# Last attention of a four-layer block on one core: the two heads of a unit are scored half a unit apart, each in banks of its own

## The reference, cut to what matters

```python
sim = jnp.einsum('bhid,bhjd->bhij', q * DIM_HEAD ** -0.5, k)      # 1024 x 1101 for a head
sim = jnp.where(full_mask[:, None, None, :], sim, max_neg)
attn = jax.nn.softmax(sim, axis=-1)
out = jnp.einsum('bhij,bhjd->bhid', attn, v)
out = layer_norm(jnp.einsum('bne,ed->bnd', out, Wout), g_o, b_o)
```

## Time and the profile before

| what | value |
|---|---|
| median of 3 runs | 2089.75 us (2084.55 to 2089.76) |
| profiled execution | 2084.4 us, its span 2082.6 us |
| last attention (first to last exponential) | 1099.6 to 1967.2 us of the span |
| TensorE busy in the span | 92% |
| VectorE, ScalarE, GpSimd busy in the span | 69%, 47%, 36% |

### The profile page before, as it was taken

How to read it: one execution, slowest core, us unless ns; L and a number is a source line. 1 busy time by engine, 2 the same in 40 slices (tenths; PEclk the granted TensorE clock), 3 DMA queues, 4 the chain that set the end, 5 groups by cost and what they waited for, 6 DMA issues and landing times.

```text
span 2082.6 us, 33216 instructions
## 1 busy us (share of the span) xinstructions
PE 1921.5 (92%) x11797; PEld 1355.2 (65%) x11797; DVE 1435.7 (69%) x2676; ACT 978.5 (47%) x2079; POOL 752.3 (36%) x1145
## 2 busy tenths in 40 slices
PE   6997799696999988997878999999999999998999
PEld 3885799542699976883565666666675666655644
DVE  5775111467344457787867999999878999998755
ACT  5672333343111252226875555555545555555455
POOL 1002111000522200000006777777656777777500
PEclk9897899898999999998989999999999999999999
DMA  3702899502489960002002333333222333333201
GB/s 115 208 2 79 273 323 333 170 1 86 163 292 321 310 228 1 1 1 86 1 13 60 82 83 82 83 83 83 72 57 72 82 82 82 82 82 81 63 1 41
DMA packets 191184, 226.87 MB, mean 109 GB/s; under 512 B 28939, under 2 KB 167085, under 8 KB 191021
## 3 DMA queue, kind: packets, MB, share of 16 engines
q1 hardware_dynamic: 183725, 201.98, 33.0%
q0 software_dynamic: 7296, 22.78, 3.3%
HBM read 127.64 MB, written 29.91 MB: 76 GB/s over the span
## 4 chain that ended last, share of the span: by engine, by line
PE 45%; ACT 6%; DVE 3%; issue 1%; POOL 0%; ACTq 0%; DVEq 0%; POOLq 0%
PE ps L640 41%; ACT w_odd L1796 4%; PE ps L1214 2%; PE ps L1215 1%; ACT arena L1785 1%; PE ps L1106 0%; DVE w_odd L2532 0%; DVE small L2410 0%; POOL arena L1908 0%; ACT out_feat L1708 0%; PE ps L1115 0%; ACT xn_tok L1651 0%; DVE small L2522 0%; ACT out_feat L1714 0%; DVE arena L2380 0%
## 5 line engine op out<-in xcount | busy, mean ns | idle before, releaser
L1908 POOL COPY arena<-w_odd 32x512 f32<-32x512 f32 x1024 | 623.7, 609 | 254.4 <-DVE w_odd L2532 202.1
L640 PE MATMUL ps<-arena,w_odd 128*128 128x128 f32 (+4 forms) x2352 | 468.2, 441 | 3.0 <-DVE arena L2202 1.2
L640 PE MATMUL ps<-arena 128*64 128x256 f32 (+4 forms) x3248 | 392.3, 370 | 8.3 <-DVE arena L2333 4.4
L640 PEld LDWEIGHTS ps<-arena 128*64 128x64 f32 (+4 forms) x3248 | 258.9, 155 | 119.5 <-issue 22.6
L2532 DVE STREAM_TRANSPOSE w_odd<-w_odd 128x1024 f32<-128x1024 f32 x256 | 317.4, 1245 | 14.6 <-ACT w_odd L1796 3.0
L1796 ACT ACTIVATE w_odd<-ps,small 128x1101 f32<-128x1101 f32 x256 | 301.6, 1179 | 48.0 <-DVE small L2522 41.0
L640 PEld LDWEIGHTS ps<-arena,w_odd 128*128 128x128 f32 (+3 forms) x2352 | 286.3, 188 | 27.9 <-issue 18.7
L1781 ACT ACTIVATE arena<-ps 77x256 f32<-77x256 f32 x128 | 48.5, 379 | 295.4 <-PE ps L1215 295.4
L2522 DVE TENSOR_REDUCE small<-ps 128x1 f32<-128x1101 f32 x128 | 166.9, 1304 | 29.3 <-PE ps L640 28.1
L1893 POOL DMA_INDIRECT token_rows<-arena x62 | 59.8, 964 | 292.3 <-DVE arena L2223 292.3
L2523 DVE TENSOR_REDUCE small<-ps 128x1 f32<-128x1024 f32 x128 | 155.4, 1214 | 0.0
(11 more groups left out here) (398 smaller groups left out, 2909.8 us busy)
## 6 DMA issues: line engine op xcount, KB each, us to landing
arena<-w_odd SPq DMA_DIRECT2D x1024, 64.0 KB
w_odd<-in_s_w SPq DMA_DIRECT2D x32, 1024.0 KB, 7.4
w_odd<-in_s_wgu SPq DMA_DIRECT2D x30, 704.0 KB, 6.1
w_even<-in_s_w SPq DMA_DIRECT2D x15, 1024.0 KB, 7.3
arena<-expert_rows_in SPq DMA_DIRECT2D x62, 130.0 KB, 4.7
w_odd<-in_s_wd SPq DMA_DIRECT2D x30, 256.0 KB, 3.6
out_feat<-in_s_wgu SPq DMA_DIRECT2D x10, 704.0 KB, 5.9
expert_rows_in<-zero_row POOLq DMA_DIRECT2D x1, 5070.0 KB, 33.2
```

The lines of the kernel that those rows point to most:

```text
L640: return pe.matmul(o, lhsT, rhs, start=start, stop=stop, **kw)
L1908: pool.tensor_copy(s6_d[u % 4][32 * j:32 * j + 32, :, 256 * i:256 * i + 256], s6_pm[u % 2][32 * i:32 * i + 32, :, 256 * j:256 * j + 256]). ...
```

## The change

- Scores: `scores(u, h)` for one head. Head 0 takes banks 0 to 2, head 1 banks 3 to 5. A head's 1024 keys now lie as 512 in partitions 0 to 63 and 512 in 64 to 127, so one head alone fills both row halves of the array. For this the queries are needed with their halves exchanged too (`s6_qs`), which SyncE makes by two DMAs for each query piece. The query tile has one buffer, no longer two.
- Mask: a matmul of ones with the mask (over the other 64 partitions) starts the sum of the 77 columns, and the context matmul adds to it. VectorE's addition and the split maximum go; it takes one maximum over 1101 columns for each head.
- Order on TensorE: head 0's scores; two pieces (odd units) or the first five tiles of `weigh` (even units); `ctx_turn(u - 1)`; head 1's scores; the last four tiles of `weigh` (even) or `sums_turn` (odd). Head 1's scores wait only for head 1's last exponential, head 0's for head 0's.
- Order on VectorE: maximum of head 0; turn of head 1 of unit u - 1; maximum of head 1; turn of head 0 of unit u.
- Key pieces are made with 64 output columns in both column halves. The inverted sums are spread by a ScalarE copy (`s6_rb`) and two transposes, no longer by matmuls. The ring has two banks (6 and 7). Pieces are made in odd units and `weigh` in even ones, one unit later than before.

```diff
-        PIECES = (("q", 0, 512), ("k", 768, S), ("v", 0, 2), ("q", 512, S), ("v", 6, NKT), ("k", 0, 512), ("v", 2, 6), ("k", 512, 768))
+        PIECES = (("q", 512, S), ("k1", 256, 512), ("v", 0, 2), ("k0", 0, 512), ("v", 6, NKT), ("q", 0, 512), ("v", 2, 6), ("k1", 0, 256))
-            return 5 + r6_no[key] % 3
+            return 6 + r6_no[key] % 2
...
+            def swapped(lo, hi):
+                for r in (0, 64):
+                    sp.dma_start(s6_qs[64 - r:P - r, lo:hi], s6_q[r:r + 64, lo:hi]).then_inc(q6_in, 16)
...
-                            last = mm(PS[:, bank, 0:hi - lo], w[:, k, c * P:(c + 1) * P], rhs, start=(k == 0), stop=(k == 1))
+                            for half in range(2):
+                                rhs = keys[:, 2 * half + lo // 256:2 * half + hi // 256]
+                                last = mm(PS[64 * half:64 * half + 64, bank, 0:hi - lo], s6_wk[:, k, w0:w0 + 64], rhs, start=(k == 0), stop=(k == 1))
...
-                    context(0).then_inc(a6_s, 1)
-                    tokens(1, 0)
-                    tokens(0, 0).then_inc(a6_s, 1)
-                    pe.wait_ge(a6_s, 4 * u + 1)
-                    context(1).then_inc(a6_s, 1)
-                    tokens(0, 1)
-                    tokens(1, 1).then_inc(a6_s, 1)
+                    mm(s6_cs[h], ones[other:other + 64], s6_mk[other:other + 64, n // 8], stop=False).then_inc(a6_m, 1)
+                    tokens(own).then_inc(a6_s, 1)
+                    tokens(other).then_inc(a6_s, 1)
+                    pe.wait_ge(a6_m, 2 * u + h + 1)
+                    mm(s6_cs[h], s6_q[own:own + 64, q0:q0 + P], s6_kx[n % 2][own:own + 64], start=False).then_inc(a6_s, 1)
...
+                        last = pe.transpose(PS[:, bank, i * P:(i + 1) * P], s6_rb[g % 2][:, 2 * i:2 * i + 2].rearrange("p a b -> p (a b)"), ident[:, :])
...
                     if u < NU:
-                        scores(u)
+                        scores(u, 0)
+                    if not even:
+                        for key in pieces_of(u):
+                            piece(key[1], key[2], free_bank(key)).then_inc(r6_mm, 1)
+                    elif 4 <= u < NU + 4:
+                        weigh((u - 4) // 2, 0, 5)
+                    if 1 <= u <= NU:
+                        ctx_turn(u - 1)
+                    if u < NU:
+                        scores(u, 1)
...
+                    if even and 4 <= u < NU + 4:
+                        weigh((u - 4) // 2, 5, NKT)
                     if not even and 3 <= u < NU + 3:
-                        weigh((u - 3) // 2)
+                        sums_turn((u - 3) // 2)
...
-                        link(dve.tensor_tensor(s6_both, s6_both, s6_mk[:, u // 64].unsqueeze(1).broadcast_to([P, 2, C]), ALU.add))
-                        dve.tensor_reduce(s6_cm[:, u % 2, 0:1], s6_both[:, 1], AX.X, ALU.max, negate=True)
...
+                        maximum(u, 0)
+                    if 1 <= u <= NU:
+                        if even:
...
+                        turn(u - 1, 1)
+                    if u < NU:
+                        maximum(u, 1)
...
+                        turn(u, 0)
```

More of the change, by code:

```diff
@@ L379, in build, with pieces_of @@
         r6_no, r6_sb, done = {}, {}, {"act": 0, "dve": 0}
+        def pieces_of(u):
+            n, j = divmod(u, 8)
+            own = [("w", n, 0)] if j == 1 and 1 <= n < 16 else []
+            return own + [("w", n + 1, i) for i in (j - 1, j) if j % 2 and i and n < 15]
         for u in range(NU + 5):
             even = u % 2 == 0
[L382 to L393, removed]
+            turn = [("c", u - 1)] if 1 <= u <= NU else []
+            if even:
+                batch = turn + ([("v", (u - 4) // 2)] if 4 <= u < NU + 4 else [])
+            else:
+                batch = pieces_of(u) + turn
+                if 3 <= u < NU + 3:
+                    batch += [("r", (u - 3) // 2)]
+                if u >= 5 and (u - 5) // 2 % 32 >= 28:
+                    batch += [("o", (u - 5) // 2)]
+                if u in N7:
+                    batch += [("n", N7[u])]
             for key in batch:
@@ L625, in _ @@
                         ld(dst, src, w_in[7])
-            for u in range(NU):
+            def swapped(lo, hi):
+                for r in (0, 64):
+                    sp.dma_start(s6_qs[64 - r:P - r, lo:hi], s6_q[r:r + 64, lo:hi]).then_inc(q6_in, 16)
+            sp.wait_ge(c6_sb, 8)
+            swapped(0, S)
+            turns = 1
+            for u in range(NU):
+                for key in pieces_of(u):
+                    kind, lo, hi = PIECES[key[2]]
+                    if kind == "q":
+                        copied(sp, key)
+                        sp.wait_ge(q6_in, 32 * turns)
+                        swapped(lo, hi)
+                        turns += 1
                 turned(sp, u)
@@ L1191, in scores @@
                     if u:
-                        pe.wait_ge(a6_p, 2 * u)
+                        pe.wait_ge(a6_p, 2 * u - 1 + h)
+                    own, other = 64 * h, 64 - 64 * h
                     q0 = qt * P
[L1194 to L1200, removed]
@@ L2507, in stage6, with maximum, turn @@
                     piece(0, j, j).then_inc(c6_sb, 1)
+                def maximum(u, h):
+                    dve.wait_ge(a6_s, 6 * u + 3 * h + 3)
+                    dve.tensor_reduce(s6_nm[:, u % 2, h:h + 1], s6_sc[h], AX.X, ALU.max, negate=True).then_inc(a6_mx, 1)
+                def turn(u, h):
+                    dve.wait_ge(a6_p, 2 * u + h + 1)
+                    dve.transpose(s6_pm[u % 2][:, h], s6_pm[u % 2][:, h]).then_inc(t6_done, 1)
                 for u in range(NU + 6):
                     even = u % 2 == 0
-                    if even and 4 <= u < NU + 4:
-                        g = (u - 4) // 2
+                    if not even and 5 <= u < NU + 5:
+                        g = (u - 5) // 2
                         c = (g // 4) % 8
@@ L2533, in stage6 @@
-                        if not even:
-                            g = u // 2
-                            if g >= 2:
-                                dve.wait_ge(r6_mm, r6_no["r", g - 2] + 1)
-                            dve.reciprocal(s6_rc[:, g % 2], s6_sm[:, g % 2]).then_inc(a6_rb, 1)
-                    if even and u >= 6 and 28 <= (u // 2 - 3) % 32 < 31:
-                        added(u // 2 - 3)
-                    if even and u >= 4 and (u // 2 - 2) % 32 >= 28:
-                        normed(u // 2 - 2)
@@ L2542, in stage6 @@
-                    if not even and u >= 5 and ((u - 1) // 2 - 2) % 32 == 31:
-                        added((u - 1) // 2 - 2)
+                        turn(u, 0)
+                    if not even and u >= 7 and 28 <= (u - 7) // 2 % 32 < 31:
+                        added((u - 7) // 2)
+                    if not even and u >= 5 and (u - 5) // 2 % 32 >= 28:
+                        normed((u - 5) // 2)
+                    if even and u >= 6 and (u - 6) // 2 % 32 == 31:
+                        added((u - 6) // 2)
```

175 lines of the change are left out of this document (93 added, 82 removed).

## The result

| | before | after |
|---|---|---|
| median | 2088.15 us (4 runs, 2084.55 to 2089.76) | 2153.69 us (4 runs, 2152.11 to 2156.94) |
| ratio | | 1.0318, 95% interval 1.0299 to 1.0338 |
| profiled execution, its span | 2084.4, 2082.6 us | 2156.94, 2155.2 us |

What follows compares the result with a forecast made beforehand. TensorE was taken as the bound: pairs go from 12.85 to 13.6 us plus 0.08 waiting, +50 over 60 pairs; with -4, +1.6 and +3 at the ends, +51, and 1.6 for the median: 2137 us, range 2090 to 2172.

Steps and rivals of the forecast that it cites:

- Bound: Last attention: TensorE, busy 99 us of 100, bounds the kernel; a pair of units holds 0.15 us of waiting.
- Scores, +0.8 a pair: TensorE's score blocks: a head costs 1.27 us where half of today's block costs 1.07, four heads a pair.
- The faster rival: Scores: a head costs only its columns and extra shape changes hide; block 1.08 with its gap, 2064 us; chance 0.10.
- Shape changes, +0.2 and +0.1: TensorE, a pair: cutting `weigh` in two costs 0.2 us (0 to 0.2), key pieces in column halves 0.1 (0 to 0.2).
- sums: `sums_turn` on TensorE: two transposes take 0.37 us for 0.59, -0.2 us a pair.
- Wait behind the piece copies, +0.08: Odd units: TensorE waits 0.15 to 0.2 us where the last piece copy is long; +0.08 a pair (0 to 0.3).
- Moves: SyncE's 8 DMAs a unit, started after the second turn: two-unit chain 12.4 us, under 13.6; slower rival 2185 us, chance 0.06.
- m: Time of SyncE's moves in the two-unit chain: between 5.3 and 9.0 us, taken as 7.0, deciding from 8.2.
- Two banks in the ring ... No cost.: Ring of result banks: each copy is needed one result earlier; nearest, `weigh`'s scaling, due after 1.5 us; no cost.
- First swap, +3 (0 to 5): Stage start: first scores wait for an uncovered swap, two issues and a landing of up to 3.6 us; 3 us taken.
- Units 120 to 123, -4: Four units without pieces: 28.85 us before, the chain of moves allows 24.8 after; -4 us.
- From unit 124 on, +1.6: Units 124 to 127 hold projections, so TensorE's longer scores count: 2 x 0.8 = +1.6 us.

Runs made afterwards that it cites:

- The first run: Changed kernel with `weigh` whole again, ahead of the turn of the context part in even units: 2305.25 us, ratio 1.1031 to the kernel before.
- the run with both early: Changed kernel with ScalarE's row-tile copy ahead of head 1's exponential and first query halves exchanged first, `weigh` in two parts: 2140.89 us, ratio 1.0245.

## Why the prediction was right, and where its terms were off

The forecast was 2137 us (+51); 2153.7 was measured (+66), inside the range.

- **Bound.** Right. TensorE was full and is full, and the waiting in a pair (0.15 us by my count, 0.13 in the mean of four pairs) is all that went. VectorE fell to 74, further than the 80 that I had. The kernel with the sums' part alone adds that the loop stood right behind TensorE.
- **Scores, +0.8 a pair.** Right: 1.27 to 1.28 a head, 5.10 for four, where two old blocks take 4.28: +0.82. The half of the old block was a good model of the new one. The faster rival asked for 1.08 and is out.
- **Shape changes, +0.2 and +0.1.** The first is +0.15, shown in both kernels. The Trainium skill (TensorEngine Tiling (Array Packing), Key Properties) says that changing the tiling mode drains TensorE; these 0.15 us, at a place where no semaphore is waited for, agree. The second hardly shows: the two pieces and their change of shape take 3.09 us for 3.07 in the mean of four pairs. The sum comes out: 12.72 + 0.82 + 0.15 - 0.21 (sums) + 0.02 (pieces) = 13.50 for a measured mean of 13.52.
- **Wait behind the piece copies, +0.08.** Absent: no plain pair has it. Plain pairs were over-estimated by 0.16 us, 4 us in units 8 to 55 and 10 us in 60 pairs. That was luck for the total: it hid a third of what the ring and the two ends cost beyond the forecast.
- **Moves.** Right. m is 7.3 us in the changed kernel (issued from 1416.36, exponential released at 1423.66) for 7.0, the exponentials wait for it 7.6 us in 200 (1350 to 1550), and in that stretch no matmul waits for an exponential. That it lies close to deciding, the run with adjacent heads shows.
- **"Two banks in the ring ... No cost."** Wrong, and the step that failed. I had checked only the results of plain pairs. In 16 units a further result takes a bank, and TensorE waits 19.1 us for the ring where it had no such wait before: 7.1 behind the row tiles' copies (shown: the early copy returns them), 7.1 behind the projections and 4.9 behind the context's copies (both read from the waits, not tried). The first run shows how narrow the ring is: with two places exchanged and the scaling left where it stood, it lost 150 us.
- **First swap, +3 (0 to 5).** Mis-sized: 8.1 us, of which the early swap returns 6.1. The fall of the clock behind the idle time was no term at all; by the run with both early it is about 2.2 us in units 0 to 7.
- **Units 120 to 123, -4.** Right: -3.4. Their four take 25.5 us for 24.8.
- **From unit 124 on, +1.6.** The largest term that was mis-sized: +14.7. I had counted the longer scores and nothing else, neither the `weigh` that comes a unit later (4.0 us, which the first stretch saves) nor the waits, most of them the ring's (5.6 us more), nor the clock behind them (3.3).
- **Open.** No run takes the stretch from unit 124 on apart; its split is read from the rows. Of the +6.4 of units 0 to 7 (like for like, with the moved `weigh` counted), 4.2 remain with the early swap, 3.3 of them the longer scores.

## What to carry to other kernels

Ask first what the engine that fills its window would win: with TensorE busy 99 us of 100, freeing VectorE could return 1%, and each matmul, cut and change of the array's shape that the freeing needs is paid in full. Where a ring of banks shrinks, list every user of it, those too that come in few units, and ask for each which engine empties it and what stands ahead of that in its queue. Look at the end of a pipelined stage as well as at its steady part: here it held more than half of the miss, with waits that no plain pair had. And take a mixed change apart: the sums' transposes alone gained 0.3% (0.2 to 0.4%), while the whole lost 3.2%.

## What was not expected of the hardware

- A 77-column pair of passes inside the row-split scores costs only 0.04 us of TensorE's time: without the mask's pair the block is 1.23 for 1.27.
- Cutting one run of 36 passes in column halves by two whole-array transposes costs 0.15 us beyond the transposes, 4.19 for 4.04, in two different kernels. Where the blocks in a row are all whole-array, two transposes take 0.22 us of TensorE between starts, for 0.37 between blocks of another shape.
- Short repeated waits cost twice. With waits of 1.9 us in the mean in 57 units the granted clock over 100 us was 0.91, and an idle time of 4.85 us, with another of 3.07 us behind it, went with a mean of 0.73 over 15 us, the first passes in it at the lower of the clock's two levels (1.2 for 2.4 GHz). Behind unit 124 waits of 1.66 and 2.28 us were followed by blocks that took 2.0 and 1.7 times as long as elsewhere.
